# Attention makes normalised token-major rows; no transposes or division of them in the FFN stage

## The reference, cut to what matters

```python
x = L0_attn_x                                   # (4, 2048, 512), float32; 16 heads of 32
q, k, v = x @ Wq.T, x @ Wk.T, x @ Wv.T          # split into heads
attn = softmax(q @ k.T / sqrt(32))              # over 2048 keys, for each head
x = layernorm(x + attn @ v)                     # heads side by side again, over 512, eps 1e-5
w = where(weights >= 0, 1, -1)
y = clip((x @ w.T) * scale + bias, -100, 100)
x = layernorm(x + y)
```

## Time and profile before

| | |
|---|---|
| median of three runs | 2723.47 us |
| profiled execution | 2722.63 us, span 2720.5 us |
| busy, share of the span | PE 99%, ACT 83%, DVE 81%, POOL 23% |
| chain that ended last | PE 97%, DVE 1%, ACT 1%, issue 1% |
| granted TensorE clock, 540 to 2440 us | 1.00 |
| granted TensorE clock, 2441 to 2471 us | 0.68 |
| granted TensorE clock, 2471 to 2696 us | 1.00 |

### The profile page before, as it was taken

The page is one execution under the profiler, slowest core; times in us unless marked ns, Lnnn a source line. Parts: engine busy times, 40 slices in busy tenths (PEclk is TensorE's granted clock), DMA queues, the critical chain, the costliest instruction groups (busy, mean ns, idle before and its releaser), DMA issues.

```text
span 2720.5 us, 92280 instructions
## 1 busy us (share of the span) xinstructions
PE 2685.3 (99%) x38720; PEld 1581.4 (58%) x38720; DVE 2193.1 (81%) x2623; ACT 2260.5 (83%) x2726; POOL 615.2 (23%) x661
## 2 busy tenths in 40 slices
PE   9999999999999999999999999999999999979998
PEld 8888888744454444444444444445455544447887
DVE  7444444379989989989989989989998998978998
ACT  5333333399999999999999999999999999965665
POOL 1000000012222222222222222222222222225665
PEclk9999999999999999999999999999999999989999
DMA  6555555589898999989899898999989899975553
GB/s 230 191 195 193 186 186 186 197 170 199 172 208 176 200 188 193 202 168 210 172 199 194 179 207 175 199 184 199 194 173 206 177 201 187 184 178 176 190 189 136
DMA packets 262711, 513.33 MB, mean 189 GB/s; under 512 B 20674, under 2 KB 135362, under 8 KB 260164
## 3 DMA queue, kind: packets, MB, share of 16 engines
q0 software_dynamic: 73440, 267.42, 52.4%
q1 hardware_dynamic: 179108, 222.61, 25.4%
q10 hardware_dynamic: 9792, 17.83, 1.7%
HBM read 122.43 MB, written 117.96 MB: 88 GB/s over the span
## 4 chain that ended last, share of the span: by engine, by line
PE 97%; DVE 1%; ACT 1%; issue 1%; DMA 0%; SPq 0%; POOL 0%; ACTq 0%; POOLq 0%; DVEq 0%
PE banks L637 34%; PE banks L669 33%; PE banks L228 19%; PE banks L1021 7%; PE banks L690 2%; PE banks L1010 1%; PE banks L1003 1%; PE banks L1017 1%; PE banks L250 0%; PE banks L1004 0%; PE banks L256 0%; DMA scratch_v<-v_out 0%; DMA score_rows<-scratch_k_lo 0%; ACT y L1039 0%; DVE qk_raw L357 0%
## 5 line engine op out<-in xcount | busy, mean ns | idle before, releaser
L780 ACT ACTIVATE probs<-banks 128x1024 f32<-128x1024 f32 x2048 | 1877.5, 1781 | 4.1 <-PE banks L637 4.1
L637 PE MATMUL banks<-score_rows 97*32 97x512 f16 x16384 | 1259.4, 382 | 4.9 <-POOL den_in L595 3.9
L669 PE MATMUL banks<-probs,v_keys 128*32 128x256 f32 x16384 | 1251.6, 379 | 0.5 <-ACT probs L780 0.5
L609 POOL DMA_DIRECT2D total<-partial x510 | 439.0, 861 | 1439.2 <-DVE partial L835 498.6
L835 DVE TENSOR_TENSOR partial<-partial,probs 128x1024 f32<-128x1024 f32 x640 | 748.4, 1221 | 0.0
L669 PEld LDWEIGHTS banks<-probs,v_keys 128*32 128x32 f32 x16384 | 510.5, 110 | 405.8 <-ACT probs L780 0.9
L831 DVE TENSOR_TENSOR partial<-probs 128x1024 f32<-128x1024 f32 x512 | 604.2, 1222 | 119.9 <-issue 109.7
L637 PEld LDWEIGHTS banks<-score_rows 97*32 97x32 f16 x16384 | 351.4, 95 | 509.7 <-ACT probs L780 413.2
L356 DVE TENSOR_TENSOR qk_lo<-banks,qk_hi 128x512 f16<-128x512 f32 x128 | 88.4, 691 | 241.7 <-ACT qk_hi L311 241.6
L311 ACT ACTIVATE qk_hi<-banks 128x512 f16<-128x512 f32 x128 | 76.0, 594 | 185.2 <-PE banks L228 185.2
L228 PE MATMUL banks<-xT_hi,w_hi 128*128 128x512 f32 x512 | 197.6, 390 | 0.0
(11 more groups left out here) (95 smaller groups left out, 2180.4 us busy)
## 6 DMA issues: line engine op xcount, KB each, us to landing
total<-partial POOLq DMA_DIRECT2D x510, 512.0 KB, 6.2
scratch_q_raw<-qk_raw SPq DMA_DIRECT2D x16, 1024.0 KB, 5.7
scratch_k_raw<-qk_raw SPq DMA_DIRECT2D x16, 1024.0 KB, 5.7
scratch_v<-v_out SPq DMA_DIRECT2D x16, 1024.0 KB, 5.1
score_rows<-scratch_q_hi SPq DMA_DIRECT2D x128, 128.0 KB, 5.5
score_rows<-scratch_k_hi SPq DMA_DIRECT2D x128, 128.0 KB, 4.3
v_keys<-scratch_v SPq DMA_DIRECT2D x64, 256.0 KB, 7.0
scratch_attn<-wf_scaled SPq DMA_DIRECT2D x64, 256.0 KB
```

Source lines behind the costliest of these rows:

```text
L609: pool.dma_start(total[:, qb % 2, heads], partial[:, g - 1, heads], accum_op=ALU.add).then_inc(a_merge[qb % 2][pair], 16)
L637: last = nc.tensor.matmul(scores_of(phase, unit)[part, i, :], k_rows[:, h, keys], q_rows[:, h, qb * BLK:(qb + 1) * BLK], start=True, stop= ...
L669: last = nc.tensor.matmul(banks[rows, out_bank(qb), cols], v_keys[:, kt, rows], probs[:, kt % P_RING, h, cols], start=(kt == 0 and part == ...
L780: nc.scalar.activation(probs[:, kt % P_RING, heads, :], scores_of(it % SLOTS, qb * UNITS + u), ACT.Exp, scale=SCALE / GAIN ** 2).then_inc( ...
```

## The change

In `attend` the denominators are made per token instead of being repeated over 32 partitions: the ones become `select`, whose piece c has ones in one column only, and the four pieces add up in the same 128 columns of the bank. The pieces stand behind tiles 8, 9, 10 and 11. DVE copies those 128 columns (`copy_den`, before the additions of tile 13), PE turns them with one 128x128 transpose behind tile 12, DVE takes the reciprocal of the 16 numbers per token (`invert_den`, behind tile 13), PE turns the copied output back into the bank with four 128x128 transposes behind tile 14 (`turn_output`), and DVE multiplies the bank by the reciprocals into `normal` behind tile 15 (`normalise`). `values` at tile 0 now wait on `a_norm`, the multiplication of two blocks before. The scratch tensor for the output is token-major, in rows of 128 features (512 bytes), and there is no scratch tensor for the denominators. In the FFN stage the five transposes, the reciprocal and the multiplication are gone; POOL adds x to the loaded rows directly. A block is loaded by four DMAs for the output and one for x.

```diff
-DEN_TILES = (8, 10, 12, 13)
-DEN_EDGES = (0, 128, 256, 384, BLK)
-OUT_AFTER = 2
-DEN_AFTER = 13
+DEN_TILES = (8, 9, 10, 11)
+TURN_TILE = 14
+DEN_TURN_TILE = 12
+OUT_AFTER, DEN_AFTER, INVERT_AFTER, NORMAL_AFTER = 2, 12, 13, 15
...
-            sp.wait_ge(a_out, it * QB + qb + 1)
-            dst = dram["attn"].rearrange("n (g p) t -> (n g) p t", p=P)[bass.ds(it, 1), :, cols]
-            sp.dma_start(dst.rearrange("o p t -> (o p) t"), out_sb[:, qb % 2, :]).then_inc(a_store[qb % 2], 16)
-            sp.wait_ge(a_dout, it * QB + qb + 1 + 2)
-            dst = dram["den"].rearrange("(i h) t -> i h t", h=G)[bass.ds(it, 1), :, cols]
-            sp.dma_start(dst.rearrange("o h t -> (o h) t"), den_sb[0:P:HD, qb % 2, :]).then_inc(a_store[qb % 2], 16)
+            sp.wait_ge(a_norm, it * QB + qb + 1 + 2)
+            dst = dram["attn"].rearrange("n g (b c q) f -> (n g) b q c f", b=QB, q=P)[bass.ds(it, 1), qb]
+            src = normal[:, qb % 2, :].rearrange("q (c f) -> q c f", c=TPB)
+            sp.dma_start(dst.rearrange("o q c f -> (o q) c f"), src).then_inc(a_store[qb % 2], 16)
...
                 if kt == 0:
-                    pe.wait_ge(a_dout, st + 1)
+                    pe.wait_ge(a_norm, st + 1)
...
+        def turn_output(it, qb):
+            st = it * QB + qb
+            pe.wait_ge(a_dout, st + 1 + 2)
+            for c in range(TPB):
+                cols = slice(c * P, (c + 1) * P)
+                last = nc.tensor.transpose(banks[:, out_bank(qb), cols], out_sb[:, cols], ident2[:])
+            last.then_inc(a_turn, 1)
...
-                    last = nc.tensor.matmul(banks[rows, out_bank(qb), cols], ones[:], part[:, h, cols],
-                                            start=(part is parts[0]), stop=(part is parts[-1]))
+                    last = nc.tensor.matmul(banks[rows, out_bank(qb), 0:P], select[:, piece, :], part[:, h, cols],
+                                            start=(piece == 0 and part is parts[0]),
+                                            stop=(piece == TPB - 1 and part is parts[-1]), skip_group_check=True)
...
+        def turn_denominators(it, qb):
+            pe.wait_ge(a_dcopy, it * QB + qb + 1)
+            nc.tensor.transpose(banks[:, out_bank(qb), P:2 * P], den_sb[:], ident2[:]).then_inc(a_dturn, 1)
...
         def copy_den(st, parity):
             dve.wait_ge(a_den, (st + 1 + 2) * len(DEN_TILES))
-            dve.wait_ge(a_store[parity], (st - parity) * 16 + 32)
-            nc.vector.tensor_copy(den_sb[:, parity, :], banks[:, out_bank(parity), :]).then_inc(a_dout, 1)
+            dve.wait_ge(a_dturn, st)
+            nc.vector.tensor_copy(den_sb[:], banks[:, out_bank(parity), 0:P]).then_inc(a_dcopy, 1)
+
+        def invert_den(st, parity):
+            dve.wait_ge(a_dturn, st + 1)
+            dve.wait_ge(a_norm, st + 2)
+            src = banks[:, out_bank(parity), P:2 * P].rearrange("q (h c) -> q h c", h=G)[:, :, 0:TPB]
+            nc.vector.reciprocal(rden[:].rearrange("q c h -> q h c"), src).then_inc(a_dout, 1)
+
+        def normalise(st, parity):
+            dve.wait_ge(a_turn, st + 1)
+            dve.wait_ge(a_dout, st + 1 + 2)
+            dve.wait_ge(a_store[parity], (st - parity) * 8 + 16)
+            nc.vector.tensor_tensor(normal[:, parity, :].rearrange("q (k d) -> q k d", d=HD),
+                                    banks[:, out_bank(parity), :].rearrange("q (k d) -> q k d", d=HD),
+                                    rden[:].rearrange("q c h -> q (c h)").unsqueeze(2).to_broadcast([P, TPB * G, HD]),
+                                    ALU.mult).then_inc(a_norm, 1)
...
-                for c in range(DC):
-                    nc.tensor.transpose(aT_bank(s)[:, c * P:(c + 1) * P], attnT[k][:, c, cols], ident3[:])
-                nc.tensor.transpose(banks[:, 6 + s % 2, 0:P], den_in[k][:, cols], ident3[:]).then_inc(f_aT, 1)
...
-                nc.vector.reciprocal(rden[:, attn_s % 2], den_bank(attn_s)).then_inc(f_rden, 1)
...
-                nc.vector.tensor_tensor(attn[:, attn_s % 2].rearrange("p (h d) -> p h d", h=H),
-                                        aT_bank(attn_s).rearrange("p (h d) -> p h d", h=H),
-                                        rden[:, attn_s % 2].unsqueeze(2).to_broadcast([P, H, HD]), ALU.mult).then_inc(f_attn, 1)
```

More of the change, by code:

```diff
@@ L704, in steps @@
                     values(it, qb, kt, half)
-                if kt in DEN_TILES and qb > 0:
-                    denominators(it, qb - 1, DEN_TILES.index(kt))
-                elif kt in DEN_TILES and not (isinstance(it, int) and it == 0):
-                    denominators(it - 1, QB - 1, DEN_TILES.index(kt))
+                if qb > 0:
+                    behind(it, qb - 1, kt)
+                elif kt < HEAD and not (isinstance(it, int) and it == 0):
+                    behind(it - 1, QB - 1, kt)
         def item(scores, it, phase):
@@ L718, in item @@
             else:
-                for piece in range(len(DEN_TILES)):
+                for piece in range(TPB):
                     denominators(it, QB - 1, piece)
+                turn_denominators(it, QB - 1)
+                turn_output(it, QB - 1)
         def all_items(scores):
@@ L818, in item, with finish_last @@
                 st = it * QB + qb
+                def finish_last(kt):
+                    if first and qb == 0:
+                        return
+                    if kt == OUT_AFTER:
+                        copy_out(st - 1, (qb - 1) % 2)
+                    if kt == DEN_AFTER:
+                        copy_den(st - 1, (qb - 1) % 2)
+                    if kt == INVERT_AFTER:
+                        invert_den(st - 1, (qb - 1) % 2)
+                    if kt == NORMAL_AFTER:
+                        normalise(st - 1, (qb - 1) % 2)
                 for kt in range(KT):
                     if kt in EDGES:
+                        finish_last(kt)
                         continue
@@ L835, in item @@
                             nc.vector.tensor_tensor(into, into, probs[:, kt % P_RING, heads], ALU.add).then_inc(a_sum[pair], 1)
-                    if kt == OUT_AFTER and not (first and qb == 0):
-                        copy_out(st - 1, (qb - 1) % 2)
-                    if kt == DEN_AFTER and not (first and qb == 0):
-                        copy_den(st - 1, (qb - 1) % 2)
+                    finish_last(kt)
         for it in range(ITEMS):
@@ L945, in load @@
             sp.wait_ge(f_res[0], b * TPB + TPB)
[L946 to L949 removed]
+            for t in range(TPB):
+                src = dram["attn"][bass.ds(batch, 1), :, bass.ds(column + t * P, P), :]
+                sp.dma_start(attn[k][:, t].rearrange("p (g f) -> p g f", g=NG), src.rearrange("o g p f -> p (o g) f")).then_inc(f_in[k], 16)
             load_x(b, k)
         load_x(0, 0)
[L953 removed]
+        sp.wait_ge(f_const, 1)
         with sp.Fori(0, ROUNDS - 1) as r:
```

102 lines of the change are left out of this document (43 added, 59 removed).

## The result

The changed kernel takes 2736.28 us, the median of five runs (2734.87 to 2737.53), where the kernel before takes 2723.27 on the same chip (five runs, 2722.12 to 2724.31). The ratio is 1.0049, 95% interval 1.0035 to 1.0063: 13.0 us slower. The forecast was 2722 us. The profiled execution has a span of 2734.5 us, 14.0 more than before.

What follows compares the result with a forecast made beforehand. ACT was taken to bound attention at 29.33 us a block, with a ring of waits at 29.47 after the change. 2722.6 + 9 (attention) - 12.7 (FFN) + 2.5 (border) = 2721.4, median 2722 us; 8-in-10 range 2708 to 2742 us.

Steps and rivals of the forecast that it cites:

- PE's added work: Attention: five transposes at 0.108 us each add 0.54 us a block, so PE still fits under ACT's 29.33 us.
- The term of +9 us: Attention: ACT waits 0.14 us in each of 63 blocks for a ring of waits of 29.47 us.
- The prediction's own sign of being wrong: Forecast wrong if attention and FFN don't move against each other, or if either moves by more than 20 us.
- The base of the load: Attention: PE's work in a block before the change, 64 groups and 4 pieces, 28.68 us.
- The ring of waits: Attention: values at tile 0, last denominator piece, DVE's copy, six additions, reciprocal, product, next values: 29.47 us against ACT's 29.33.
- The FFN stage: Without transposes, product and reciprocal a step falls from 4.01 to 3.815 us; -12.7 us in all.
- the two paths: FFN stage: two dependency paths through a step, 3.72 and 3.91 us, each starting where the other ends, 3.815 us a step.
- The border: From attention's end to the FFN stage: longer final compute, bigger store and more loads, +2.5 us, ends 0 and +5.
- A: Rival, slower: attention's ring of waits is longer than summed, 29.75 us a block, 2740 us; chance 0.23.
- B: Rival, faster: the ring stays within ACT's attention block and the FFN gives its 12.7 us, 2713 us; chance 0.25.
- C: Rival, faster still: B, and the FFN stage is bound by PE at 3.47 us a step, 2694 us; chance 0.06.
- D: Rival, slower by much: attention transposes between 32-column matmuls cost 0.27 us each, PE 30.03 us a block, 2757 us; chance 0.08.

Runs made afterwards that it cites:

- e3: The changed kernel with the four transposes of the output made twice in the same place, 8 instead of 4: 2761.9 us, ratio 1.0147 to the kernel before.
- e8: The kernel before with five transposes added to PE's list, one behind tile 5 and four behind tile 7, nobody waiting for them: 2750.2 us, ratio 1.0100.
- e11: The changed kernel with the output's four transposes split, two behind tile 5 and two behind tile 14: 2750.4 us, ratio 1.0098 to the kernel before.
- after: The changed kernel itself, as measured against the kernel before: 2736.3 us, ratio 1.0049.
- e9: The changed kernel with the denominators turned by one ordinary 128-wide matmul of 16 moving columns instead of a transpose: 2741.9 us, ratio 1.0071 to the kernel before.
- e12: The changed kernel with all five transposes behind tile 13, reciprocal and product behind tile 14 (reciprocals wrong in value): 2721.4 us, ratio 0.9994 to the kernel before.
- e1: The changed kernel without the 5 transposes of each attention block, waits, copies and product kept (output wrong): 2720.6 us, ratio 0.9992 to the kernel before.
- e7: e1 with the product one tile earlier, behind tile 14 instead of 15: 2711.7 us, ratio 0.9958 to the kernel before.
- e10: The changed kernel with denominators made per token by 64 one-moving-column matmuls a block instead of 16, without their transpose: 2825.8 us, ratio 1.0374 to the kernel before.

## Why the prediction was wrong

The step that failed is the one on PE's added work: "Five are 0.54 us: PE has 28.68 + 0.54 = 29.22 of 29.33 us. That still fits, with 0.11 us left." The 0.108 us for each transpose is right, in the attention too (e3). It was read in the FFN stage, where all neighbours are 128 wide. In the attention all neighbours are 32 wide, and each of the two places costs 0.25 to 0.30 us on top (e8, e11). The five cost 1.10 us, the load is 29.78, above ACT's 29.33. The term of +9 us became +27.9. The prediction's own sign of being wrong, a stage that moves by more than 20 us, is met. The span moved by +14.0 us where -1.2 was forecast: the attention came out 18.9 us worse, and FFN stage and border together 3.6 us better.

- **The base of the load**, 28.68 us, was right: added to the visits that each trace shows, it gives the block within 0.05 us in six of the kernels that the load binds (after, e3, e8, e9, e11, e12).
- **The ring of waits** was sized right (29.47 against 29.46 in e1), in part by luck: in e1 the values start 0.15 us behind the product's end and not 0.04, and the copy, the six additions and the reciprocal took 7.12 us and not 7.21. But it is hidden in the changed kernel, because PE arrives later than the ring does. Without the transposes it costs 2720.6 - 2711.7 = 9 us (e1 against e7), the very term. It was the second limit, not the first.
- **The FFN stage** has two steps in turn, of 3.86 and 3.67 us, with PE waiting 0.17 us for ACT's rows in the longer one, as the two paths said. Its step is 3.752 on the mean instead of 3.815: from the first clip to the last it is 14.4 us less, where 12.7 were forecast. The one step in the trace of before was a little longer than those of a steady run.
- **The border** costs 1.2 us at the first residual and 0.6 at the first clip, not 2.5. The copy, the reciprocal and the product took what was said.
- **The rivals.** A's time (2740, block 29.75) is nearest, but its mechanism isn't what bound: no PE wait for the product. B and C needed the load to fit; B's number came true in e7. D is right in its kind, transposes that cost more between matmuls of 32 columns, and wrong in its law: not 0.27 for each, but 0.108 for each and about 0.27 for each place. By D's law e11 would have been as fast as the changed kernel and e3 slower by 4 x 0.27 x 63 = 68 us; it was 26.

The row that carried the warning was there: PE had 0.65 us to spare in a block, and the price of a 128-wide matmul among 32-wide ones stands in no row of before. The prediction treated it as one number with the ends 0.108 and 0.27, and gave the upper end 0.08; a cost per place was not among the ends.

The Trainium skill has a rule that bears on this, in another place than I had looked: TensorEngine Tiling (Array Packing), Tiling Modes, Key Properties says that a change of the tiling mode, unlike a change of the tile, drains TensorE. The runs agree: the denominators' pieces, which change the tile and the weights but stay 32 wide, cost no more than their own 0.22 us, and each change to 128 wide and back costs 0.25 to 0.30 us, a number that the page doesn't give. That this time is such a drain is not shown: the runs tie it to the change of width and don't look inside it. The figure that the prediction weighed is about 275 ns for a 128x128 transpose of bf16 numbers in a kernel (the Trainium skill, TensorE: Matmul & The Clock Gate, Part 4: PE-mode transpose). The trace agrees for the time in work of one, 0.27 us, but it is not what a transpose costs in a row of them here: 0.108 us.

## What to carry to other kernels

Price an instruction where it will stand, not where it stands now: here a start-to-start distance held only among neighbours of the same width. On PE, count the places at which the width of the stationary tile changes, and put the 128-wide work of a block into one place, or make it 32 wide if its moving side is short (here 16 columns: 0.06 us against 0.47). When an engine has a few tenths of a microsecond left in a block, sum its load to the end before working out a ring of waits: the longer of the two decides, and the other costs nothing until the first is mended.

## What the runs showed of the hardware

- A visit of 128-wide matmuls among 32-wide ones costs 0.25 to 0.30 us beside the work: 0.37 to 0.41 us for one transpose of 128x128, 0.47 for two, 0.69 for four, 0.79 for one and four in two groups, 1.12 for eight. By the medians of 46 to 94 such places in each run, 0.10 to 0.15 us of it stand before the first 128-wide matmul and 0.15 between the last one and the next scores (after, e3, e8, e11). The weight load at its head is late by 0.41 us in the profile, with "issue" as the reason.
- DVE's reciprocal of 128x512 out of PSUM takes 3.36 us, and of 128x16 0.25 us: (3.36 - 0.25)/496 = 6.3 ns a column, against 0.69 us for a copy or product of 512. The Trainium skill, VectorE: DVE Perf Modes, First, the fixed hardware budget, says that the reciprocal runs as an iterative division with a repeat count of 8. The trace agrees in kind: a column costs 6.3 ns where a copy's costs 0.61 us/512 = 1.2.
- 48 matmuls more in a block (e10) brought gaps of up to 3.3 us on PE that the profile can't explain.
